# A graph layer whose edge sums are placed once per group of 1 to 16 steps instead of once per step

## The reference, cut to what matters

```python
xn = _layernorm(x, axis=-1)
support = segment_sum(edge_weight[:, None] * xn[src], dst, num_segments=6250)
x = x + (support @ weight + bias) + linear_attention(xn)
x = x + ffn(_layernorm(x))
```

## Time and profile before

| what | us |
|---|---|
| three runs | 1811.52 (median), 1809.19, 1826.64 |
| span of the profiled execution, first to last instruction | 1612.4 |
| what lies around the span, by the median | 199.1 |
| PE busy / DVE / ACT / POOL | 1470.5 / 1144.0 / 702.1 / 865.2 |

### The profile page before, as it was taken

How to read it: one execution, slowest core, us unless ns; L and a number is a source line. 1 busy time by engine, 2 the same in 40 slices (tenths; PEclk the granted TensorE clock), 3 DMA queues, 4 the chain that set the end, 5 groups by cost and what they waited for, 6 DMA issues and landing times. The chain is left out here.

```text
span 1612.4 us, 27387 instructions
## 1 busy us (share of the span) xinstructions
PE 1470.5 (91%) x8552; PEld 651.6 (40%) x8552; DVE 1144.0 (71%) x2341; ACT 702.1 (44%) x1143; POOL 865.2 (54%) x882
## 2 busy tenths in 40 slices
PE   4988979999999999899999999989996999889994
PEld 2544433333333333334444444434443444543331
DVE  7978736655665665568888888878887666356787
ACT  5787633332233333224433333333335777434453
POOL 0002277777777777777777777777762554110000
PEclk9999989999999999999999999999997999999996
DMA  7899688888888888877777777787776445436774
GB/s 228 290 314 347 233 250 260 257 258 253 254 261 261 262 262 255 287 210 238 236 236 238 236 235 237 235 258 235 241 209 203 161 160 215 140 112 213 238 247 146
DMA packets 163486, 379.43 MB, mean 235 GB/s; under 512 B 26437, under 2 KB 32215, under 8 KB 163363
## 3 DMA queue, kind: packets, MB, share of 16 engines
q0 software_dynamic: 62720, 205.57, 42.1%
q1 hardware_dynamic: 99923, 171.27, 30.9%
q10 hardware_dynamic: 720, 1.06, 0.2%
HBM read 300.77 MB, written 78.23 MB: 235 GB/s over the span
## 5 line engine op out<-in xcount | busy, mean ns | idle before, releaser
L1079 POOL DMA_INDIRECT rows<-y_rows,idxT x516 | 499.9, 969 | 172.1 <-issue 166.2
L1414 DVE SCALAR_TENSOR_TENSOR acc<-bank,maskt,acc 128x512 f32 x392 | 276.1, 746 | 173.8 <-PE bank L1971 128.3
L846 ACT ACTIVATE mb<-bank,ones,ncols 128x512 f32<-128x512 f32 x98 | 76.4, 779 | 369.2 <-PE bank L1860 369.2
L1971 PE MATMUL bank<-part,plc 128*128 128x512 f32 x392 | 212.2, 624 | 0.7 <-ACT part L840 0.7
L840 ACT COPY part<-bank 128x512 f32<-128x512 f32 x196 | 113.0, 576 | 142.9 <-PE bank L1961 142.6
L1860 PE MATMUL bank<-Wg,xtb 128*128 128x512 f16 x588 | 138.8, 387 | 14.2 <-ACT xtb L803 7.5
L1860 PE MATMUL bank<-Wk,xta 128*128 128x512 f16 x588 | 139.4, 388 | 0.0
L1860 PE MATMUL bank<-Wq,xta 128*128 128x512 f16 x588 | 137.8, 385 | 0.0
L1860 PE MATMUL bank<-ztg,G 128*128 128x512 f16 (+1 forms) x624 | 135.9, 370 | 0.0
L1860 PE MATMUL bank<-KVP,qT 128*128 128x512 f16 x588 | 135.4, 380 | 0.0
L1961 PE MATMUL bank<-rows,hots 128*32 128x512 f16 x1548 | 114.0, 400 | 20.1 <-DMA rows<-y_rows,idxT 18.6
(11 more groups left out here) (313 smaller groups left out, 2398.5 us busy)
## 6 DMA issues: line engine op xcount, KB each, us to landing
xta<-xt_rows SPq DMA_DIRECT2D x98, 256.0 KB
x_rows<-xhl SPq DMA_DIRECT2D x49, 256.0 KB, 3.5
xt_rows<-xtb SPq DMA_DIRECT2D x49, 256.0 KB, 3.7
y_rows<-yb SPq DMA_DIRECT2D x49, 256.0 KB, 3.5
xr<-x_rows SPq DMA_DIRECT2D x49, 256.0 KB, 4.3
z_rows<-zn SPq DMA_DIRECT2D x49, 256.0 KB, 2.0
zt_rows<-ztg SPq DMA_DIRECT2D x49, 256.0 KB, 2.0
zq<-z_rows SPq DMA_DIRECT2D x49, 256.0 KB, 2.7
```

The costliest lines, as they stand in the source:

```text
L846: nc.scalar.activation(mb[:, :], of[:, :], ACT.Relu, scale=ncols[:, col:col + 1], bias=ones[:, 0:1]).then_inc(f_min, 1)
L1079: pool.indirect_dma_start(out=row_slot(s, k).rearrange("p a d -> p (a d)"), out_offset=None, in_=y_rows, in_offset=bass.IndirectOffsetOnAx ...
L1414: nc.vector.scalar_tensor_tensor(out=flat(acc, tile + m), in0=placed_bank(s)[:, :], scalar=maskt[:, m, s:s + 1], in1=flat(acc, tile + m), ...
L1971: nc.tensor.matmul(placed_bank(s)[:, :], plc[:, s // WG % 3, s % WG, :], part32[:, s % 2, :], start=True, stop=True).then_inc(placed, 1)
```

## The change

The 196 steps are cut into 98 groups: 1 group of 16 steps, 3 of 8, 9 of 4, 35 of 2 and 50 of 1, in this order. In a group of m steps, quarter k holds m consecutive sub-groups, 128 m sorted edges, and the m steps add to the same PSUM bank; step i of the group takes sub-group i of each quarter. `keep_part`, `place` and `add_group` happen once, behind the group's last step. The gathers and the 12 matmuls of each step stay, in number and order of homes; which sub-group a gather fetches differs. The offsets of an edge are now measured from the first edge of its quarter, so SP loads that number for every sub-group (`qfirst`), and `srow` has one number per quarter of a group, 392 instead of 784. The edge lists are loaded as 98 partitions of 1024 edges instead of 112 of 896.

```diff
+RUNS = ((16, 16), (8, 24), (4, 36), (2, 70), (1, 50))
...
+NGP = len(LONG)
+GROUP_OF = [n for n in range(NGP) for _ in range(LONG[n])]
-EC = 7
+EC = 8
...
+def ending(s):
+    if 0 <= s < NGR and (s + 1 == NGR or GROUP_OF[s + 1] != GROUP_OF[s]):
+        return GROUP_OF[s]
...
+def subgroup(s, k):
+    n = GROUP_OF[s]
+    return K4 * FIRST[n] + LONG[n] * k + s - FIRST[n]
...
 (gathers, POOL)
-                    e = K4 * s + k
+                    e = subgroup(s, k)
...
 (head tables, DVE)
-                    dve.wait_ge(edges_loaded, 16 * 12)
+                    dve.wait_ge(edges_loaded, 16 * EDGE_LOADS)
...
-                        in1=per(dstL)[:, :, 0:1].broadcast_to([EP, EC, P]), op0=ALU.add, op1=ALU.subtract))
+                        in1=qfirst[0:EP, :].rearrange("p (c e) -> p c e", e=1).broadcast_to([EP, EC, P]), op0=ALU.add, op1=ALU.subtract))
...
 (part, PE)
-                        ins = nc.tensor.matmul(edge_bank(s)[W * i:W * i + W, :], hots[:, k, p, :, m + i],
-                                               row_slot(s, i)[:, q, :], start=n == 0, stop=n == len(PASSES) - 1)
+                        ins = nc.tensor.matmul(edge_bank(n)[W * k:W * k + W, :], hots[:, r, p, :, hot_column(s, k)],
+                                               row_slot(s, k)[:, q, :], start=s == FIRST[n] and i == 0,
+                                               stop=ending(s) is not None and i == len(PASSES) - 1, skip_group_check=True)
...
 (place, PE; keep_part and add_group alike)
-                if not 0 <= s < NGR:
+                n = ending(s)
+                if n is None:
                     return
-                pe.wait_ge(part_kept, s + 1)
-                pe.wait_ge(placing, s // WG + 1)
+                pe.wait_ge(part_kept, n + 1)
+                pe.wait_ge(placing, n + 1)
```

More of the change, by code:

```diff
@@ L36 @@
 NSG = K4 * NGR
-EC = 7
+RUNS = ((16, 16), (8, 24), (4, 36), (2, 70), (1, 50))
+LONG, FIRST = [], []
+for m, slots in RUNS:
+    for _ in range(slots // m):
+        FIRST.append(sum(LONG))
+        LONG.append(m)
+NGP = len(LONG)
+GROUP_OF = [n for n in range(NGP) for _ in range(LONG[n])]
+EC = 8
 EP = NSG // EC
@@ L56 @@
 SLOTS_END = max(NGR + 2, Q_FIRST + Q_SPACE * (T - 1) + 7)
+EDGE_LOADS = 3 * 3 + 1 + len(RUNS) + 1 + 3 + sum(EC // m if m <= EC else K4 * slots // m for m, slots in RUNS[:-1])
 KEYS_END, LINES_AT, BASE_AT, GATE_AT = TURN - 7, TURN + 9, TURN + 12, NGR - 31
@@ L117, in gather_count, with ended, hot_column @@
     return sum(gather_sem(i) == gather_sem(s) for i in range(s + 1))
+def ending(s):
+    if 0 <= s < NGR and (s + 1 == NGR or GROUP_OF[s + 1] != GROUP_OF[s]):
+        return GROUP_OF[s]
+def ended(s):
+    return sum(ending(i) is not None for i in range(min(s, NGR - 1) + 1))
+def subgroup(s, k):
+    n = GROUP_OF[s]
+    return K4 * FIRST[n] + LONG[n] * k + s - FIRST[n]
+def hot_column(s, k):
+    return K4 * (s % WG) + k if LONG[GROUP_OF[s]] == 1 else WG * k + s % WG
 def last_user(home):
@@ L258, in build @@
             ("relL", [P, EC * P], F32))
[L259 to L260 removed]
+        srow, srowf = (nc.alloc_sbuf_tensor_at("srow", [1, K4 * NGP], I32, offset=rI),
+                       nc.alloc_sbuf_tensor_at("srowf", [1, K4 * NGP], F32, offset=rI + 4 * NSG))
         bf, bfq, b16, brow, xnb, pad = over(
@@ L552, in load_edges @@
                 real = -(-E // P)
-                sp.dma_start(srow[:, 0:real], flat_dst[:, 0:E:P]).then_inc(edges_loaded, 16)
-                sp.dma_start(srow[:, real:NSG].rearrange("p (n b) -> p n b", b=1), last_dst.broadcast_to([1, NSG - real, 1])).then_inc(edges_loaded, 16)
+                at, col = 0, 0
+                for m, slots in RUNS:
+                    n = K4 * slots // m
+                    have = min(n, (real - at) // m)
+                    sp.dma_start(srow[:, col:col + have], flat_dst[:, at * P:min(E, (at + have * m) * P):m * P]
+                                 ).then_inc(edges_loaded, 16)
+                    at, col = at + n * m, col + n
@@ L1259, in edge_targets @@
                     dve.wait_ge(edges_turned, 1)
[L1260 to L1266, removed]
+                    wide = bank[0][:, 0:K4 * NGP]
+                    for k in range(K4):
+                        q = slice(W * k, W * k + W)
+                        link(nc.vector.tensor_scalar(maskt[q, 0, :], by_group(wide)[q, :, k], quadf[q, 0:1], None,
+                                                     ALU.add))
                 if part == 2:
@@ L1269, in edge_targets @@
                     link(nc.vector.tensor_tensor(tgt[:, :], maskt[:, 0, :], maskt[:, 1, :], ALU.add))
[L1270 to L1274, removed]
+                    first = bank[0][:, K4 * NGP:(K4 + 1) * NGP]
+                    for m, op in enumerate((ALU.is_le, ALU.is_gt)):
+                        link(nc.vector.tensor_scalar(maskt[:, m, :], first, stepf[:, 0:1], mscale[:, 0:1], op, ALU.mult))
                     dve.nop(nofuse=True).then_inc(edge_ints, 1)
@@ L1379, in _, with place_matrix @@
             head_ticks(head_tick, T + 3)
[L1382 to L1390, removed]
+            def place_matrix(n):
+                at_least(dve, placed, n - 3 * WG + 1)
+                nc.vector.tensor_scalar(plc[:, n % (3 * WG), :], iota16[:, :], tgt[:, n:n + 1], None, ALU.is_equal
+                                        ).then_inc(placing, 1)
             def hot_pair(w):
@@ L1596, in _ @@
                 else:
-                    place_pair((s + 1) // WG)
+                    for end in range(s + 1, s + 1 + WG):
+                        n = ending(end)
+                        if n is not None:
+                            place_matrix(n)
                 for slot_of, after, work in ((k_slot, 1, k_whole), (q_slot, 1, q_shares)):
@@ L1867, in spread_starts @@
                 pe.wait_ge(edge_ints, 2)
[L1868 to L1873 removed]
+                nc.tensor.matmul(bank[0][:, 0:K4 * NGP], ones[0:1, :], srowf[:, :], start=True, stop=True)
+                nc.tensor.matmul(bank[0][:, K4 * NGP:(K4 + 1) * NGP], ones[0:1, :], wofff[:, :], start=True, stop=True
+                                 ).then_inc(edges_turned, 1)
             def turn_edges(n):
```

121 lines of the change are left out of this document (75 added, 46 removed).

## The result

The changed kernel takes 1797.1 us (median of 18 runs, 1791.9 to 1808.6), the kernel before 1814.1 (18 runs, 1796.6 to 1826.6): a ratio of 0.9916, 95% interval 0.9897 to 0.9936. That is 0.84% less, clear of noise but no change by the prediction's bound of 1%. The forecast said 1808 and no change. Both held, but not for its reasons, and the first line of the profile says so: the profiled execution took 1805.6 us, of which its span is 1803.8. Nothing like 199 us lies around it.

A forecast was written before the change was run, and what follows sets the result against it. The prediction took POOL's back-to-back gathers to bound the edge phase. From 1811.5 us, waits -2.2, placements 0, tables -2, loads +1 and end 0 sum to -3.2, so 1808 us; range 1789 to 1825.

The forecast's parts named there:

- The frame: Whole kernel: a span of 1612.4 us and 199.1 us around it, 1811.5 in all, as the base of the forecast.
- The edge phase is POOL's: Edge phase: POOL writes 784 gathers one after another at 1.251 us, 980.8 us, and PE waits for them.
- theory Q: An experiment's expectation: each gather occupies something PE's announcements share for 1.48 to 1.51 us, so a line grows 0.25 us a gather.
- Placements, copies and adds cost nothing: Edge phase: 98 placements (100 us of PE), 196 adds (146 us of DVE) and 98 copies go, hidden by POOL's pace: 0.
- PE sets the pace: Rival, edge phase: PE is the bound, so 100 us go, 1711 us; chance 0.04.
- POOL's waits: Edge phase: POOL's 2.54 us wait for PE in slot 96 goes, -2.2 us, between -2.2 and +6.
- collisions with `kl`: Key stretch: `kl` lengthens gathers by 16.3 us, taken as unchanged (-16 to +8); rival without them 1789 us, chance 0.08.
- Head: Before the first gather: smaller DVE table operations -2 us (0 to -3.6), 18 more edge loads +1 (0 to about 7).
- End: Behind the last gather: nothing changes as the last 50 groups are single steps, 0, between -3.2 and 0.
- The prediction's own signs: Right: gathers some 1000 us, PE busy about 100 us less. Wrong: POOL waiting for `partial_done`, DVE empty at first edge table.
- PE goes slow: Rival, key stretch: idler PE gets a lower clock, over 1% slower below about 0.74; chance 0.08 together with stalling loads.

The follow-up runs named there:

- r1_before: The kernel before, unedited, profiled again: 1813.7 us, ratio 0.9992.
- p3_light: The changed kernel with one pass instead of three in the key, query, key-value and mix products: 1775.9 us, one run.
- p4_thin: The kernel before with 32 columns instead of 512 in each of its 196 placements: 1814.8 us, ratio 0.9996.
- p5_thin3: The kernel before with 32 columns instead of 512 in placements, copies of partial sums and adds of placed sums: 1794.4 us, ratio 0.9989.
- h3_two: The changed kernel with two gathers a step instead of four: 1492.5 us, one run.
- h3_twob: The kernel before with two gathers a step instead of four: 1580.8 us, one run.
- h4_homes: The changed kernel with half rows (1 KB) gathered and twice the buffers: 1814.6 us, one run.
- p1_pause: The changed kernel with two dependent memsets on POOL ahead of each step's four gathers: 1809.0 us, ratio 0.9967.

## Why the prediction was right, and where its steps failed

**The frame failed.** "Against 1612.4 us of span and 199.1 around it, 1811.5 in all": 1.8 us lie around the span (1813.8 us of time and 1812.0 of span in r1_before's profiled execution). The profiled execution shown was of another kind than those timed: with the same kernel, its announcements of PE took 0.04 us and its stretch 1.277 us a gather. Its trace also holds more records of semaphores, 26790 updates against 15551 in r1_before, of the same program. Whether that is a cause or a sign no run shows, nor whether taking the trace has a part in PE's delays: none compares an execution with and without it.

**"The edge phase is POOL's" failed as a mechanism, and held as a result.** The step 784 x 1.251 us, one gather after another with hardly a wait, is wrong: POOL stops 100 times. What binds is a limit of 1.48 to 1.52 us a gather that POOL's own pace undercuts; POOL, PE, bytes, rows and buffers were each changed by much and moved it by 0.04. So the forecast of no change was in part luck: the gathers do cover the placements, but by a limit that the prediction did not know. That PE's announcements stand in one line with the gathers, and are late because it grows, is an inference, and a plain line does not give the sizes. In p3_light the product that ended at 587.5 was heard of within 0.04 us, so no line stood then; at the 0.25 us a gather of theory Q the six gathers up to 594.6 make 1.5 us, and the next announcement took 15.5. What the runs show is the limit, that lateness and PE's breaks go away when gathers are halved, and that the median lateness goes when they are paced (the mean hardly does: 1.94 us after 2.32).

**"Placements, copies and adds cost nothing"** was right of their time, with the wrong cover: p4_thin and p5_thin3 show nothing gained, h3_two against h3_twob shows the 88 us that appear once gathers are no longer the limit. That is the first rival, *PE sets the pace*, 100 us by its own sum; it got 0.04 and would have been right with half the gathers.

**POOL's waits** were sized at -2.2 us, with +6 as the other end. Measured, one profiled execution each: stops 226.8 to 207.6, -19.2; the gathers' own time, where the collisions with `kl` were to show, 751.8 to 756.6, +4.7 (0 forecast, -16 to +8); the usual gaps +2.9. The stretch gets 11.6 us shorter. It all stands ahead of step 146, where the groups of one begin (-12.8); behind it the two kernels are alike (+1.3). Such a split is good to some 6 us only: p4_thin and p5_thin3, neither of which gains by its ratio, have stretches of 1195.3 and 1183.2.

**Head** (-2 for tables, +1 for loads): the first gather starts 2.9 us later, 208.3 against 205.4, in these two executions. In the seven other runs with the changed kernel's head it starts at 202.4 to 206.1, in the five with the head of before at 203.6 to 205.4, so the start did not move beyond its scatter. The loads were mis-sized where they stand, though. SP's rows, to be laid beside the earlier trace rows, and DVE's first edge table:

```profile
18.34 0.63 SPq L590 DMA_DIRECT2D srow<-in_dst  x1
19.01 1.34 SPq L613 DMA_DIRECT2D qfirst<-in_dst  x4
20.39 2.48 SPq L607 DMA_DIRECT2D qfirst<-in_dst  x7
22.91 0.85 SPq L598 DMA_DIRECT2D qfirst<-in_dst  x1
...
26.53 1.23 DVE L1281 SCALAR_TENSOR_TENSOR relL<-dstL,qfirst 98x1024 f32<-98x1024 int32 x1 [2.53 <-DMA qfirst<-in_dst]
```

The next row, the load of x, comes at 25.26, against 19.99 in r1_before; twenty loads took 0.54 us each from start to start, in the middle between the two prices and not near the cheap end, and DVE's first edge table starts at 26.53 instead of 24.07, after an empty stretch of 2.53 us. **End**: from the last gather's end 418.6 and 419.1 us, 0 as forecast, though this tail lies anywhere from 405 to 427 us in the runs. In all -11.6 + 2.9 + 0.5 = -8.2, the difference of the two spans. The medians differ by 17: the changed kernel's profiled execution, 1805.6 us, is 8.5 above its median, so these rows account for half of the gain only.

**The prediction's own signs** said so. Of those for right, gathers of some 1000 us from first to last did not come (1188.0 and 1176.4), nor PE's busy time lower by about 100 (1549.3 to 1511.5 us, 38 less). Of those for wrong, POOL did wait for `partial_done`, and DVE's first edge table had its empty stretch.

**PE goes slow** did not decide: the mean granted clock over the span was 0.945 before and 0.918 after, and 0.815 in p3_light, the shortest with all gathers.

## What to carry to other kernels

Lay the profiled span beside the timed runs first: where they differ by more than a few us, profile the kernel again before reasoning from the rows, rather than carry the difference along as a constant. Where engines hand work to each other, measure from the producer's end to the consumer's start; a producer's own rows don't show that its announcement is late. And work taken off an engine is worth its time only where that engine sets the pace: the 98 placements were worth 88 us with half the gathers, and with all of them the whole change brought 17.

## What the runs showed of the hardware that was not expected

While POOL writes indirect gathers at 1.25 us each, announcements of PE come up to 16 us late in p3_light and 36 in h4_homes, whether PE is busy or idle, and in bursts; ACT's and DVE's stay within 0.04 us at the median. PE also stands still inside runs of matmuls that wait for nothing, for 31 us (p1_pause) to 97 us (h4_homes) in all. A gather costs 1.48 to 1.52 us then, with 128 rows or 64, rows of 2 KB or 1 KB; at 2.2 to 2.4 us a gather (h3_two, h3_twob) nothing is late and no run of matmuls breaks up. In the profile shown ahead of the prediction neither happened at 1.277 us a gather. What PE shares with the gathers, and what sets that execution apart, is open.
